# A graph kernel that gathers node rows: items of two chunks, rows as high and low halves, and a preparation that goes group by group

## The chip, the cores and the metric

The kernel runs on one core of a Trainium2 chip (trn2). The metric is the device time of one execution in microseconds. Before the change it is 2641.29 us, the median of 3 runs (2641.16 to 2641.54).

## What is computed

6250 nodes have 256 features each (x), and 200000 edges (src, dst) are sorted by their destination. With xn the layer norm of x, the result is

```python
x = x + gnn(edges, xn) + mix(xn)      # gnn: relu(segment_sum(h[src]*dinv[src]*dinv[dst], dst) + b), h = xn @ W, with self loops
x = x + ffn(layernorm(x))             # mix: linear attention over all nodes, two layer norms, a GELU layer
                                      # ffn: 8 experts, top-1 routing with a capacity, 256 -> 1024 -> 256
```

dinv is one over the square root of a node's number of incoming edges, its self loop among them. All values are float32.

## The kernel before

The nodes are 49 blocks of 128, the edges 1563 chunks of 128 consecutive edges (NCHUNK). The program has four stages, one after the other: `prepare`, `aggregate_and_mix`, `route` and `experts`. The change touches the first two.

`prepare` makes the table `node_rows` in DRAM, one row of 256 float32 per node (1024 bytes), which holds h times dinv of the node. ScalarE normalises a block of x (L455), TensorE transposes it (L530), ScalarE copies the transpose (L462), TensorE multiplies it by W in four records of a float32 product (L537), and ScalarE stores the result in `acc` (L471, L468). VectorE computes means and variances (L363, L364) of seven blocks at a time, called a group. The degrees come from the sorted destinations: GpSimd gathers one row of 128 destinations for each of the 49 blocks (`crow`, L303), VectorE counts in it (`compare`, L380 and L383), and from the places of the block ends (L396), shifted by one node on TensorE (L554, L555), come the degrees (L401) and dinv (L405 to L409). This is done once, for all 49 blocks together, when all `crow` rows have landed. 40 blocks have been stored without dinv by then and are scaled by VectorE (L413), nine are stored with it. SyncE writes the table in four transfers. At the end come the item lists: for 13 tiles of 128 chunks ScalarE, TensorE and VectorE turn the edge lists into columns (`src_chunk`, `dst_item`) and into the number of the chunk of every item (`chunk_item`, L436 to L440).

`aggregate_and_mix` does the edges. An item is one pair of a chunk and a block that has destinations in it; there are 1611. For every chunk GpSimd gathers the 128 rows of its sources with one indirect DMA (L680) into a slot of `ring`, which holds 32 chunks. Four chunks are a gang. SyncE waits until gang k has landed and raises `ready`, then waits until gang k-4 has been multiplied and raises `free`, for which GpSimd waits before it reuses the slots. For every item VectorE makes a 128x128 matrix of zeros and ones by comparing a column of destinations with 0 to 127 (`select`, L917), TensorE multiplies it with the gathered rows (L702, a float32 product in two records), and VectorE adds the result to the block's rows in `acc` (`add`, L930), four items later. Passes of 21 items (PER) hold the rest of the work between the items at fixed places: first the keys and values (four blocks per pass, 13 passes), then the attention and the hidden layer (one block per pass, 50 passes), then items alone. SyncE also fills `expert_rows` with empty rows, 7.9 MB in one transfer at gang 20 (L668), and a small one for the rest.

The order on each engine is that of the program; engines wait for one another by counting semaphores.

## Time and profile before

| | |
|---|---|
| median of 3 runs | 2641.29 us |
| the profiled execution's own time | 2633.95 us |
| its span | 2632.2 us |
| mean granted clock of TensorE | 0.864 |
| TensorE busy (matmul) | 1953.6 us, 74% |
| VectorE busy | 1718.5 us, 65% |
| ScalarE busy | 837.1 us, 32% |
| GpSimd busy | 1786.2 us, 68% |
| gathers of node rows | 1563 |

The times of the instructions come from the profiled execution, counted from the start of its span. Its own time is 1.75 us longer than its span and 7.34 us below the median of the other runs. Matmul records of one product overlap, so their mean duration is longer than the distance between two. "Issue" before an instruction is time in which its engine waited for nothing that the profile shows.

### The profile page before, as it was taken

The numbers are of one execution on the slowest core, as the hardware profiler recorded it, in microseconds if no ns is written. First come the engines' busy times: TensorE is split into PE (matmuls) and PEld (weight loads), VectorE is DVE, ScalarE is ACT, GpSimd is POOL, SyncE is SP. The second block draws the span as 40 slices with busy tenths as digits, with TensorE's granted clock in tenths as the row PEclk, the third lists the DMA queues.
The fourth block names the chain that finished last, engine by engine and source line by source line (L and its number), as shares of the span: only waits on it lengthen the run. The fifth ranks groups of instructions, "written<-read, shape, count | busy, mean of one in ns | idle before, by whom it ended". The sixth has DMA issues, their size and how long they took to land. (4 is left out here: it accounts for less than half of the span.)

```text
span 2632.2 us, 41321 instructions
## 1 busy us (share of the span) xinstructions
PE 1953.6 (74%) x8589; PEld 1434.4 (54%) x8589; DVE 1718.5 (65%) x5672; ACT 837.1 (32%) x1670; POOL 1786.2 (68%) x1893
## 2 busy tenths in 40 slices
PE   6785987777677777777767677766666575999996
PEld 4453554555455554555555455534333364888886
DVE  6553665666766666666666767655555593888885
ACT  5431332233233333333333333300000064544542
POOL 6276777777777777777777777777777553355354
PEclk9898999788888888888898978987777755999998
DMA  6336333333333333333333333333333333212320
GB/s 192 123 107 218 105 107 105 105 105 106 106 105 106 105 105 106 105 106 106 105 106 105 106 105 105 106 105 106 105 106 106 95 126 134 74 60 68 105 69 8
DMA packets 137976, 278.31 MB, mean 106 GB/s; under 512 B 34578, under 2 KB 81825, under 8 KB 137626
## 3 DMA queue, kind: packets, MB, share of 16 engines
q0 software_dynamic: 82144, 218.73, 28.6%
q1 hardware_dynamic: 55610, 57.09, 6.7%
q8 instruction: 83, 1.36, 0.2%
q14 instruction: 139, 1.14, 0.1%
HBM read 244.19 MB, written 35.50 MB: 106 GB/s over the span
## 5 line engine op out<-in xcount | busy, mean ns | idle before, releaser
L680 POOL DMA_INDIRECT ring<-node_rows,src_chunk x1563 | 1484.9, 950 | 483.0 <-issue 475.5
L702 PE MATMUL p_item<-ring,sel 128*128 x3222 | 1094.2, 469 | 543.6 <-SPq L650 438.8
L702 PEld LDWEIGHTS p_item<-ring,sel 128*128 128x128 f32 x3222 | 644.6, 225 | 907.3 <-issue 835.1
L930 DVE TENSOR_TENSOR acc<-acc,p_item 128x256 f32 (+1 forms) x1611 | 676.1, 420 | 668.7 <-PE p_item L702 596.6
L917 DVE TENSOR_SCALAR sel<-col,dst_item 128x128 f32<-128x128 f32 x1611 | 493.4, 307 | 0.5 <-PEq L167 0.5
L1437 POOL TENSOR_TENSOR low<-low,big 128x256 f32<-128x256 f32 x64 | 56.2, 879 | 173.0 <-DVE big L1617 172.5
L1551 PE MATMUL e_y<-w2h,hTh 128*128 128x256 f32 x512 | 148.7, 290 | 2.4 <-DVE hTl L1603 2.0
L1551 PE MATMUL e_y<-w2h,hTl 128*128 128x256 f32 x512 | 143.1, 279 | 0.0
L1551 PE MATMUL e_y<-w2l,hTh 128*128 128x256 f32 x512 | 142.9, 279 | 0.0
L1244 ACT ACTIVATE sdg<-mvg,eps_ln 128x7 f32<-128x7 f32 x7 | 2.1, 302 | 368.7 <-DVE mvg L1167 368.6
L1538 PE MATMUL e_f<-bTh,w1h 128*128 128x490 f32 (+1 forms) x256 | 99.8, 390 | 2.7 <-ACT hbuf L1486 2.7
L1551 PEld LDWEIGHTS e_y<-w2h,hTh 128*128 128x128 f32 x512 | 96.3, 188 | 4.4 <-DVE hTl L1603 3.8
L1538 PE MATMUL e_f<-bTh,w1l 128*128 128x490 f32 (+1 forms) x256 | 98.7, 385 | 0.0
L1538 PE MATMUL e_f<-bTl,w1h 128*128 128x490 f32 (+1 forms) x256 | 98.6, 385 | 0.0
L1486 ACT ACTIVATE hbuf<-e_f,fb_sb 128x490 f32<-128x490 f32 (+1 forms) x128 | 79.5, 664 | 57.1 <-DVE hTl L1603 36.4
L1428 POOL DMA_INDIRECT out_dram<-oo,rows x64 | 79.4, 1240 | 25.9 <-DVE oo L1594 16.8
L1551 PEld LDWEIGHTS e_y<-w2l,hTh 128*128 128x128 f32 x512 | 96.5, 188 | 0.0
L1551 PEld LDWEIGHTS e_y<-w2h,hTl 128*128 128x128 f32 x512 | 96.2, 188 | 0.0
L767 PE MATMUL p_q<-wq_sb,xnT_m 128*128 128x512 f32 x196 | 94.8, 607 | 0.0
L1123 POOL DMA_INDIRECT expert_rows<-acc,dest x49 | 57.6, 1176 | 52.6 <-DVE dest L1218 39.8
L853 ACT ACTIVATE x1T<-p_t,col_ln1b,col_ln1g 128x128 f32<-128x128 f32 x98 | 39.5, 453 | 169.1 <-PE p_t L733 169.1
L847 ACT ACTIVATE x1n<-t_m,nm,r 128x256 f32<-128x256 f32 x49 | 29.4, 600 | 179.0 <-DVE nm L980 179.0
(246 smaller groups left out, 2918.6 us busy)
## 6 DMA issues: line engine op xcount, KB each, us to landing
ring<-node_rows,src_chunk POOLq DMA_INDIRECT x1563
w1raw<-in_w SPq DMA_DIRECT2D x8, 1024.0 KB, 6.8
w2raw<-in_w SPq DMA_DIRECT2D x8, 1024.0 KB, 5.6
expert_rows<-empty SPq DMA_DIRECT2D x1, 7930.0 KB
rows<-expert_rows SPq DMA_DIRECT2D x8, 910.0 KB
res<-in_x SPq DMA_DIRECT2D x7, 896.0 KB, 11.0
out_dram<-acc SPq DMA_DIRECT2D x7, 896.0 KB, 4.1
node_rows<-acc SPq DMA_DIRECT2D x2, 1792.0 KB, 7.6
```

The lines of the kernel that those rows point to most:

```text
L680: nc.gpsimd.indirect_dma_start(ring[:, c % RING, :], None, table, bass.IndirectOffsetOnAxis(src_chunk[:, c:c + 1], 0)).then_inc(gathered[c ...
L702: pe.matmul(p_item[i % PSLOT][:, 0:C], sel[:, i % SELR, :], ring[:, bass.ds(c % RING, 1), :].rearrange("p a c -> p (a c)"), start=True, st ...
L767: mm = pe.matmul(p_kv, xnT[:, a, :], wq_sb[:, a, C:3 * C], start=(a == 0), stop=(a == CH - 1))
L853: nc.scalar.activation(x1T[:, a, :], p_t[:, a, :], ACT.Identity, scale=g["cols"]["ln1g"][:, a:a + 1], bias=g["cols"]["ln1b"][:, a:a + 1]). ...
L917: nc.vector.tensor_scalar(sel[:, i % SELR, :], col[:], dst_item[:, i:i + 1], None, ALU.is_equal).then_inc(selected, 1)
L930: nc.vector.tensor_tensor(a, a, p_item[j % PSLOT][:, 0:C], ALU.add).then_inc(added, 1)
L1123: nc.gpsimd.indirect_dma_start(slots, bass.IndirectOffsetOnAxis(dest[:, b:b + 1], 0), acc[:, b, :], None, bounds_check=SLOTS - 1, oob_is_e ...
L1428: nc.gpsimd.indirect_dma_start(out, bass.IndirectOffsetOnAxis(rows[0:r, u, t, C + 3:C + 4].bitcast(I32), 0), oo[0:r, t % 2, :], None, boun ...
L1437: nc.gpsimd.tensor_tensor(low[0:r, t % 2, :], low[0:r, t % 2, :], big[0:r, t % 2, :], ALU.add).then_inc(pool_st, 1)
L1486: nc.scalar.activation(hbuf[:, j % 2, h * NH[0]:h * NH[0] + NH[h]], p_f[(2 * j + h) % 4][:, 0:NH[h]], ACT.Relu, bias=fb1_sb[:, bass.ds(e, ...
L1538: mm = pe.matmul(p_f[c % 4][:, 0:NH[h]], w[:, a, j * P:(j + 1) * P], b[:, a, h * NH[0]:h * NH[0] + NH[h]], start=(q == 0), stop=(q == len( ...
L1551: mm = pe.matmul(p_y[t % 2][:, 0:C], h[:, j, t * P:(t + 1) * P], w[:, j, :], start=(q == 0), stop=(q == len(parts) - 1))
```

## The change

In `aggregate_and_mix` an item becomes a pair of two chunks and a block: 782 pairs, 830 items. The gathers stay one per chunk, but a row of the table is now 2048 bytes: the high half of each value (rounded to the format of single-pass products) and then the low half, the rest. An item is four single-pass products of 128x128 by 128x256 that add up in PSUM (two chunks, two halves). `select` makes two matrices in one operation, `add` stays one per item. The ring holds 24 chunks (6 gangs), KEEP and LAG are 3, SELR is 8, and a pass has 12 items with the other work at new places. The fill of `expert_rows` becomes 62 transfers of 128 rows, one at every fourth gang from gang 20.

In `prepare` the weights are centred (their column mean is taken off), so that x is transposed as it is and the product is scaled by rstd times dinv when it is stored. The counting of `crow`, the degrees and dinv go group by group, in eight groups, each before the stores of its blocks. ScalarE stores each block twice, rounded (high half) and full (`acc`), and VectorE subtracts for the low half. The halves stand in two buffers of four blocks (PIECE), and SyncE writes the table in 13 pieces. ScalarE waits for the piece two before to be written. The edge lists are transposed at the seams of groups 1 to 4, and the pair numbers come from one comparison and 13 products with a column of ones.

```diff
-PER = 21
+PER = 12
-NITEM = NCHUNK + NBLK - 1
+NITEM = NPAIR + NBLK - 1
-RING = 32
-SELR = 16
+RING = 24
+SELR = 8
-KEEP = 4
-LAG = 4
+KEEP = 3
+LAG = 3
-    table = nc.dram_tensor("node_rows", (NPAD, C), F32, kind="Internal").ap()
+    table = nc.dram_tensor("node_rows", (NPAD, 2 * C), F32, kind="Internal").ap()
...
+    CB = [0, 7, 14, 21, 28, 35, 42, 46, NBLK]
+    HELD = 3
+    PIECE = 4
+        def known(gi):
+            return (CB[gi] - 1 if gi else 0), (CB[gi + 1] - 1 if gi + 1 < NC else NBLK)
+        wanted = [max(CB[gi] - 1, 0) + HELD for gi in range(NC - 1)]
...
+            for k in range(NPIECE):                       # SyncE
+                lo, hi = k * PIECE, min(k * PIECE + PIECE, NBLK)
+                sp.wait_ge(high_ok, hi)
+                sp.wait_ge(low_ok, hi)
+                sp.dma_start(table[lo * P:hi * P, :].rearrange("(b p) c -> p b c", p=P),
+                             halves[:, k % 2, 0:hi - lo].rearrange("p b u c -> p b (u c)").bitcast(F32)
+                             ).then_inc(dma_tab[k % 2], 16)
...
+            centre_weights()                              # VectorE
+            means(0)
+            inverse_std(0)
+            means(1)
+            means(2)
+            inverse_std(1)
+            inverse_std(2)
+            for gi in range(NC):
+                positions(gi)
+                if gi + 3 < NG:
+                    means(gi + 3)
                 if gi > 0:
+                    low_halves(gi - 1)
+                degrees(gi)
+                if gi + 3 < NG:
+                    inverse_std(gi + 3)
+                inverse_degrees(gi)
+                if gi == NTB:
+                    pairs_passed()
+                if gi == NTB + 1:
+                    pair_numbers()
+            low_halves(NC - 1)
...
+            def store(b):                                 # ScalarE
                 s.wait_ge(h_ok, b + 1)
+                s.wait_ge(dinv_ok, group_of(b) + 1)
+                k = b // PIECE
+                wait(s, dma_tab[k % 2], 16 * (k // 2))
+                nc.scalar.activation(half(b, 0), h_slot(b), ACT.Copy, scale=rowscale[:, b:b + 1]).then_inc(high_ok, 1)
+                nc.scalar.activation(acc[:, b, 0:C], h_slot(b), ACT.Copy, scale=rowscale[:, b:b + 1]
+                                     ).then_inc(h_out, 1)
...
+            for b in range(NBLK):
+                copy(b)
+                if b in (1, 2):
+                    root(b)
+                for gi in range(NC - 1):
+                    if b == wanted[gi]:
+                        if gi + 3 < NG:
+                            root(gi + 3)
+                        if 1 <= gi <= NTB:
+                            as_floats(gi - 1)
+                        root_degree(gi)
+                        if 1 <= gi <= NTB:
+                            edge_columns(gi - 1)
+                if HELD <= b < NBLK - 1:
+                    store(b - HELD)
...
+            for b in range(NBLK):                         # TensorE
+                transposes(b)
+                if b > 0:
+                    products(b - 1)
+                for gi in range(NC - 1):
+                    if b == wanted[gi]:
+                        shift(gi)
+                        if 1 <= gi <= NTB:
+                            edge_columns(gi - 1)
+                        if gi == NTB + 1:
+                            pair_numbers()
...
-                pe.matmul(p_item[i % PSLOT][:, 0:C], sel[:, i % SELR, :],
-                          ring[:, bass.ds(c % RING, 1), :].rearrange("p a c -> p (a c)"),
-                          start=True, stop=True).then_inc(multiplied, 1)
+                rows = ring[:, bass.ds(q % (RING // 2), 1), :, :].rearrange("p a u c -> p (a u) c").bitcast(F32R)
+                for u in range(2):
+                    for part in range(2):
+                        mm = pe.matmul(p_item[i % PSLOT][:, 0:C], sel[:, i % SELR, u, :],
+                                       rows[:, u, part * C:(part + 1) * C], start=(u == 0 and part == 0),
+                                       stop=(u == 1 and part == 1))
+                mm.then_inc(multiplied, 1)
...
-                nc.vector.tensor_scalar(sel[:, i % SELR, :], col[:], dst_item[:, i:i + 1], None, ALU.is_equal
-                                        ).then_inc(selected, 1)
+                dst = dst_chunk[:, bass.ds(pair[i % (2 * QUAD)] * 2, 2)]
+                nc.vector.scalar_tensor_tensor(
+                    sel[:, i % SELR, :, :], dst.rearrange("p (u e) -> p u e", e=1).broadcast_to([P, 2, P]),
+                    nbase[:, bass.ds(block_of(i), 1)],
+                    col[:].rearrange("p (u e) -> p u e", u=1).broadcast_to([P, 2, P]), ALU.subtract, ALU.is_equal
+                    ).then_inc(selected, 1)
...
-                if k == 20:
-                    full = SLOTS // P
-                    sp.dma_start(slots[0:full * P, :].rearrange("(a p) c -> p a c", p=P),
-                                 empty[:].rearrange("p (a c) -> p a c", a=1).broadcast_to([P, full, ROW])
-                                 ).then_inc(dma_empty, 16)
-                    sp.dma_start(slots[full * P:SLOTS, :], empty[0:SLOTS - full * P, :]).then_inc(dma_empty, 16)
+                if k >= 20 and k % 4 == 0 and (k - 20) // 4 < NFILL:
+                    lo = (k - 20) // 4 * P
+                    rows = min(P, SLOTS - lo)
+                    sp.dma_start(slots[lo:lo + rows, :], empty[0:rows, :]).then_inc(dma_empty, 16)
```

## Rows read from the trace of the kernel before

**Rows 1.** The page's costliest groups: line, engine, operation, names, count, busy us, mean ns, idle before.

```profile
L680 POOL DMA_INDIRECT ring<-node_rows,src_chunk x1563 | 1484.9, 950 | 483.0 <-issue 475.5
L702 PE MATMUL p_item<-ring,sel 128*128 x3222 | 1094.2, 469 | 543.6 <-SPq L650 438.8
...
L930 DVE TENSOR_TENSOR acc<-acc,p_item 128x256 f32 (+1 forms) x1611 | 676.1, 420 | 668.7 <-PE p_item L702 596.6
L917 DVE TENSOR_SCALAR sel<-col,dst_item 128x128 f32<-128x128 f32 x1611 | 493.4, 307 | 0.5 <-PEq L167 0.5
```

**Rows 2.** Timeline of GpSimd: start us, length us; first gather, around 250 us, last.

```profile
121.27 1.03 POOL L680 DMA_INDIRECT ring<-node_rows,src_chunk  x1
...
245.22 0.95 POOL L680 DMA_INDIRECT ring<-node_rows,src_chunk  x1 [0.30 <-issue]
253.48 0.94 POOL L680 DMA_INDIRECT ring<-node_rows,src_chunk  x1 [7.32 <-SPq L657]
...
2087.98 0.95 POOL L680 DMA_INDIRECT ring<-node_rows,src_chunk  x1 [0.30 <-issue]
```

**Rows 3.** Operations by tile: minimum, median and maximum ns; landing of the 512-byte gathers.

```profile
L680 POOL DMA_INDIRECT ring<-node_rows,src_chunk x1563: 942/946/1194, 121.3 to 2088.0; - x196
...
L303 POOL DMA_INDIRECT crow<-in_dstR,chunk_i x49: 940/944/1709, 12.6 to 77.8; - x49
...
DMA to landing us min/median/max: 2.4/2.5/5.9
...
L1123 POOL DMA_INDIRECT expert_rows<-acc,dest x49: 971/973/3585, 2121.3 to 2205.1; - x49
```

**Rows 4.** Stretches: length, busy us (count) by engine, clock, DMA share, GB/s.

```profile
225.00:250.00 25.00, 5.60 (x22) 3.42 (x22) 4.80 (x16) 2.15 (x6) 16.08 (x17) 0.65 0.94 311
400.00:1000.00 600.00, 443.14 (x1764) 315.11 (x1764) 395.66 (x1467) 190.83 (x344) 454.68 (x478) 0.86 0.37 105
```

**Rows 5.** Timeline of SyncE's queue: the fill of the expert rows.

```profile
228.94 24.04 SPq L668 DMA_DIRECT2D expert_rows<-empty  x1
```

**Rows 6.** Groups by line from 400 to 1900 us.

```profile
L935 DVE SCALAR_TENSOR_TENSOR qT<-p_q,qe 128x256 f32<-128x256 f32 x49 | 19.9, 407 | 0.0
```

**Rows 7.** Timeline of TensorE in the experts' stage.

```profile
2400.11 0.28 PE L1551 MATMUL e_y<-w2l,hTh 128*128 128x256 f32 x1
2400.22 0.28 PE L1551 MATMUL e_y<-w2h,hTl 128*128 128x256 f32 x1
```

**Rows 8.** Timeline of the preparation, all engines' instructions by start.

```profile
12.56 1.13 POOL L303 DMA_INDIRECT crow<-in_dstR,chunk_i  x1 [9.00 <-DVE chunk_i L357]
...
82.61 0.21 DVE L396 SCALAR_TENSOR_TENSOR place<-chunk_f,count 128x49 f32<-128x49 f32 x1
...
85.50 0.21 DVE L409 TENSOR_TENSOR dinv<-dinv,tmp 128x49 f32<-128x49 f32 x1
...
86.50 0.47 ACT L468 ACTIVATE acc<-p_h,dinv 128x256 f32<-128x256 f32 x1
...
86.87 0.59 ACT L455 ACTIVATE xn<-res,nmr,rstd 128x256 f32<-128x256 f32 x1
...
87.20 1.91 PE L537 MATMUL p_h<-gw_sb,xnT 128*128 128x256 f32 x4
...
93.42 1.03 PE L537 MATMUL p_h<-gw_sb,xnT 128*128 128x256 f32 x4
...
119.78 0.27 DVE L440 TENSOR_SCALAR chunk_item<-p_row 1x128 int32<-1x128 f32 x1
```

**Rows 9.** Timeline of VectorE in the routing stage: seven statistics.

```profile
2101.47 2.38 DVE L1164 BATCH_NORM_STATS2 stt<-acc 128x6 f32<-128x256 f32 x7
```

**Rows 10.** Groups by line from 0 to 121 us: counting of a group.

```profile
L380 DVE TENSOR_TENSOR less<-crow,node_n 128x896 bf16<-128x896 int32 x7 | 7.7, 1105 | 14.0 <-DMA crow<-in_dstR,chunk_i 14.0
L383 DVE TENSOR_REDUCE count<-less 128x7 f32<-128x896 bf16 x7 | 7.6, 1086 | 0.2
```

**Rows 11.** DMA issues: count, KB each, median us to landing.

```profile
node_rows<-acc SPq DMA_DIRECT2D x2, 1792.0 KB, 7.6
```

More of the change, by code:

```diff
@@ L483, in _ @@
-            root(0)
-            root(1)
-            group(0, False)
-            with s.Fori(1, SG) as gi:
-                root(gi + 1)
-                group(gi, False)
-            for gi in range(SG + 1, NG):
-                root(gi)
-            s.wait_ge(deg_ok, 1)
-            nc.scalar.activation(dinv[:], deg[:], ACT.Sqrt).then_inc(deg_std, 1)
-            s.wait_ge(dinv_ok, 1)
-            for gi in range(SG, NG):
-                group(gi, True)
-            copy(NBLK - 1, GR - 1)
@@ new lines, in store, with as_floats @@
+                k = b // PIECE
[3 more added lines that the diff above has]
+                                     ).then_inc(h_out, 1)
+            def as_floats(k):
+                lo, hi = tiles(k)[0], tiles(k)[-1] + 1
+                s.wait_ge(dma_rows, 32)
+                for rows in (src_rows, dst_rows):
+                    nc.scalar.copy(rows[:, lo:hi, :].bitcast(F32), rows[:, lo:hi, :]).then_inc(rows_ok, 1)
@@ L508, in _ @@
+            root_degree(NC - 1)
+            for b in range(NBLK - HELD - 1, NBLK):
+                store(b)
+            s.wait_ge(listed, 2 * NTB)
         @block.tensor
@@ L524, in _, with transposes @@
             t_.wait_ge(dma_gw, 16)
-            def transposes(b, u):
-                t_.wait_ge(xn_ok, b + 1)
-                wait(t_, xnT_ok, b if u == 0 else b - 1)
+            for a in range(CH):
+                mm = pe.matmul(p_h[0][:, 0:C], ones[:], gw_sb[:, a, :], start=(a == 0), stop=(a == CH - 1))
+            mm.then_inc(mean_ps, 1)
+            t_.wait_ge(consts, 25)
+            def transposes(b):
+                t_.wait_ge(dma_x[b // GR], 16)
+                wait(t_, xT_ok, b - 1)
@@ L536, in products @@
                 for a in range(CH):
-                    mm = pe.matmul(p_h[u % 2][:, 0:C], xnT[:, u, a, :], gw_sb[:, a, :], start=(a == 0),
+                    mm = pe.matmul(h_slot(b), xT[:, b % GR, a, :], gw_sb[:, a, :], start=(a == 0),
                                    stop=(a == CH - 1))
                 mm.then_inc(h_ok, 1)
-            def group(gi):
-                for u in range(GR):
-                    b = gi * GR + u
-                    transposes(b, u)
-                    if not (isinstance(b, int) and b < 1):
-                        products(b - 1, (u - 1) % GR)
@@ L687, in _ @@
             t_.wait_ge(dma_w, 16 * NDMA_W)
-            regs = [t_.alloc_register(f"item_chunk{i}") for i in range(QUAD)]
-            chunk = []
+            regs = [t_.alloc_register(f"item_pair{i}") for i in range(QUAD)]
+            pair = []
             def item(it, k):
```

500 lines of the change are left out of this document (247 added, 253 removed).

## The prediction, made before the changed kernel ran

> **What bounds the kernel now.** I read the page first, then the timeline of GpSimd, the stretches with their DMA share, and last the first 121 us instruction by instruction. In the page's costliest groups the reader is to see that GpSimd issues one gather after the other and waits for nothing: 1563 gathers of 950 ns, and 475.5 us of "issue" between them, so 1.25 us from one to the next, 1968 us in all [rows 1]. TensorE waits most for SyncE, which signals that a gang has landed, and VectorE for TensorE. VectorE's two groups of item work fill 1170 of these 1968 us, TensorE's one 1094; neither sets the pace. The gathers run from 121.3 to 2088.9 us [rows 2], so the run is 121 us of preparation, 1968 us of gathers, and 543 us of routing and experts that nothing here touches. One edit can matter for each: when the first gather starts, what one gather costs, and what interrupts them. That an item now does two chunks halves work that is hidden.
>
> **The gathers.** Their number stays 1563. Each now fetches 128 rows of 2048 bytes. The trace has no such gather, so I bound it. Below: the 512-byte gathers of the preparation have a median of 944 ns, the 1024-byte ones 946 ns [rows 3]; on that line another 1024 bytes cost 4 ns, 6 us over 1563, or nothing if the 2 ns are noise. I take 2 us. Above: the scatter of 1040-byte rows has a median of 973 ns [rows 3], 27 ns more, which is 42 us if bytes were the reason. Since doubling once changed nothing, I stay at the low end.
>
> The bytes themselves: the gathers occupy the DMA engines 0.37 at 105 GB/s [rows 4], so twice the bytes is 0.74 if a byte keeps its price. A 512-byte gather lands 2.5 us after its issue [rows 3]. The ring shrinks from 8 gangs to 6, and with KEEP at 3 gang m is issued when gang m-3 has landed and gang m-6 is multiplied: 10 us of slack for landing, where there were 15. At 0.37 x 1.25 = 0.46 us more of transfer a gather stays far inside 10 us.
>
> The fill of the expert rows is one transfer of 24 us [rows 5]. It holds the gathers back so that GpSimd stands 7.3 us, the only stall in the stage [rows 2]. The 62 pieces of 130 KB, one every four gangs (20 us), are each under half a microsecond at the 311 GB/s of that stretch [rows 4]; the stall goes: -7.3 us. The same fill would cost it back if the engines ran at 1.0.
>
> Mean against median: 950 and 946 ns, and 944 for the gathers next to other work. (950-944) x 1563 = 9.4 us are lengthenings spread over the stage. The select, a one-input f32 operation at 307 ns [rows 1], becomes one scalar_tensor_tensor per item, and adds are halved. If these are what lengthens gathers, up to 9.4 us return; if not, none. I take 4. The Trainium skill, "SBUF — State Buffer", section "SBUF: two separate sides", says that a VectorE operation in a 2-port mode shuts GpSimd out so that it can't write descriptors, which would make the select a brake and the new form a release. The medians 944 and 946 speak against more than the 9.4 us.
>
> **Item work, hidden.** VectorE: 420 + 307 ns twice per pair of chunks [rows 1] becomes 420 plus a 128x256 scalar_tensor_tensor, 407 ns in this stage [rows 6]; 0.83 of each 2.36 us. TensorE: four single-pass products; such products follow each other in 0.12 us in the last stage [rows 7], 0.47 us per item, 0.94 at the lower of TensorE's two clock levels, against 2.36. The attention work per block moves from 21 slots of 1.22 us to 12 of 2.35, 28 us per pass in place of 26, with the same distances in time. 63 passes of 70 are used, so it ends before the gathers. Without that cover, one microsecond per pass would be 50 us. Cost: 0. The last pair adds about 0.5 us behind the last gather, since twice the bytes must land: +0.5.
>
> **The preparation.** Removed: 49 normalisations on ScalarE, 40 scalings on VectorE, and the item lists, thirteen tiles one after the other behind everything else, whose last operation ends at 120.05 us [rows 8]. Added: a second store per block on ScalarE (the high half), 49 subtractions on VectorE (the low half), eight rounds of positions, degrees and roots in place of one, and a table of 12.8 MB instead of 6.4. The chunk rows (49 gathers, the first at 12.56 us [rows 8], now without constants among them) end at 12.6 + 49 x 1.25 = 74 us and land by 76. The chain that I expect to end last is not that one but ScalarE's stores, which may start for a group only when its degrees are known:
>
> Start: after chunk_i at 12.3 us (the first chunk-row gather follows it) VectorE centres the weights (2.5 us with TensorE's product), then means of groups 0, 1, 2 (seven statistics in 2.38 us [rows 9] and seven short aggregates, an estimated 3 us each), three inverse deviations (1 us each), positions of group 0 (1.1 + 1.1 [rows 10] + 0.3), means of group 3, another deviation and the inverse degree: 12.3+2.5+9+3+2.5+3+1+1.2 = 34.5. First store at 35 us.
>
> Stores: two of 0.37 us from start to start and a copy of 0.27 (the spacing of such operations, 86.50 to 86.87 [rows 8]) is 1.01; TensorE needs about 1.2 per block (a product's four records take 1.03 when its clock is high [rows 8], and two transposes), against which three results are held. I take 1.11: 49 x 1.11 = 54.4 us.
>
> Seven seams between groups. At each, TensorE finishes the product that the last store freed (1.0), then does the shift (0.5), VectorE the degree (0.2), ScalarE the root (0.3), VectorE five linked steps of 0.2, and in four of them TensorE's eight transposes of the edge lists and ScalarE's two copies of 512 columns (1.3 + 1.2) come before the next store. The same steps over all blocks took 82.61 to 85.71 [rows 8]. So 4.4 us at four seams, 3.4 at two, 4.3 at the last: 28.7.
>
> Buffer of the halves: a piece of four blocks needs the piece two before it written out. VectorE makes low halves only after positions and means of the next group (5.5 us), and 1 MB takes 3 us plus 2 to land (1.8 MB: 7.6 [rows 11]). I place stalls at blocks 12 (2.9), 32 (3.4) and 40 (1.2): 7.5 us.
>
> End: low half 0.5, the last 1.25 MB 5.4, and 0.7 to the first gather. Sum 35+54.4+28.7+7.5+6.6 = 132.2. TensorE's clock: after the 5 us gap before 86 us its products take 1.91 us for four records and only from 93 on 1.03 [rows 8]; six seams with 3 us of idle bring some of this, +3.5 us. First gather at 136, bounds 125 (no stalls of the buffer, full clock) and 150 (every block at 1.4 us). Against 121.3: +14.7, from +4 to +29.
>
> **Sum**, against the profiled execution's own 2633.95 us: +14.7 -7.3 -4 +2 +0.5 = +5.9, 2639.9. The median of the runs is 7.3 above that execution, so 2647.2 for it.
>
> **Rivals.**
> *Preparation as fast as its gathers.* If a seam costs little, seven blocks (7.8 us) fit into the 8.75 of their seven gathers, and the end is 76 + about 8 for the last group + 6.6 = 91 to 105 at the first gather: -16 to -30. The list work that now ends at 120 speaks for it, since it is truly gone from the end. Against it: the seams are linked steps on three engines in order. It decides below 1.0 us per seam. With -8.8 in the stage: 2602 to 2617.
> *The descriptors cost by bytes.* 27 ns or more per gather: +42 us and up, about 2690. The equal medians speak against.
> *The wait moves to landing or to the block chain.* If a byte costs more than now, so that a gather's transfer passes 1.25 us (0.74 becomes 1.0), every gather follows it; 5% above is 98 us, 2740. Likewise if a pass of 12 slots needs more than 28.2 us; at 29 it is +40 us, 2690.
> *The change of select frees GpSimd.* All 9.4 us return: 2642; this lies inside my range. By the page of the Trainium skill named above this, or more, is to be expected.
> *No stall in the buffer and full clock:* 11 less than my forecast, 2636, the lower end of the spread.
>
> **How the numbers follow.** My forecast with its spread (preparation +4 to +29, stage -17 to -1): 0.72, its own range 2631 to 2668. Fast preparation 0.12. Bytes, landing or block chain 0.12. The other 0.04 is for what I have not seen. About 0.2% (5.3 us) is what a measurement tells from no change. Of the 0.72, 0.40 lies above 2646.6, 0.25 within, 0.07 below 2636. With the rivals and the rest: slower 0.40 + 0.12 = 0.52, same 0.25 + 0.02 = 0.27, faster 0.07 + 0.12 + 0.02 = 0.21. To leave out no more than 2 in 10 the range takes the slower half of the fast preparation: 2612 to 2670.
>
> **What would show it.** First gather at 136 us; ScalarE waiting for VectorE's dinv about 3 to 4 us seven times; waits of ScalarE on the node_rows DMA at blocks 12, 32, 40; gathers at 945 to 950 ns with 0.30 between; no stall near 250 us; DMA share near 0.75. I am wrong if the first gather starts before 120, if gathers are longer than 960 ns, or if GpSimd waits for SyncE again and again.

## The result, and the profile after

The changed kernel takes 2663.53 us (median of 4 runs, 2660.85 to 2664.48), the kernel before beside it on the same chip 2641.22 us (4 runs, 2637.89 to 2641.54). The ratio is 1.0086, 95% interval 1.0068 to 1.0103: slower by 22.3 us. I had forecast 2647 with a range of 2612 to 2670, and gave "slower" 0.52. The side and the range hold, but the sum is 16 us short. The profiled execution's own time is 2660.85 us, its span 2659.0 us, 26.8 us more than the 2632.2 us of before. The sum of the forecast, +5.9, was a sum of profile times, so in those it is 20.9 us short; the profiled execution of before lay 7.3 us below the median of its runs, that of the changed kernel 2.7.

First the page's costliest groups of the changed kernel, which answer to [rows 1].

```profile
L738 POOL DMA_INDIRECT ring<-node_rows,src_chunk x1563 | 1502.4, 961 | 537.6 <-issue 476.2
L763 PE MATMUL p_item<-ring,sel 128*128 x3320 | 821.1, 391 | 718.6 <-SPq L714 656.3
...
L998 DVE TENSOR_TENSOR acc<-acc,p_item 128x256 f32 (+1 forms) x830 | 345.8, 417 | 459.4 <-PE p_item L763 456.5
L987 DVE SCALAR_TENSOR_TENSOR sel<-dst_chunk,nbase,col 128x256 fp32r<-128x256 f32 x830 | 399.4, 481 | 143.4 <-issue 84.4
```

GpSimd is the bound as before: 1563 gathers with 476 us of issue between them. But a gather is 961 ns on the mean where it was 950 [rows 1], and the sum of their busy time went from 1484.9 to 1502.4 us. The two VectorE groups of item work fell from 1170 to 745 us, and nothing came of it, since they were hidden.

The operations by tile (minimum, median, maximum in ns, first and last start), against [rows 3]; then one stretch against [rows 4] (length, busy by engine, clock, DMA share, GB/s).

```profile
L738 POOL DMA_INDIRECT ring<-node_rows,src_chunk x1563: 942/949/1212, 135.8 to 2113.4; - x196
...
DMA to landing us min/median/max: 3.3/3.7/5.9
...
L353 POOL DMA_INDIRECT crow<-in_dstR,chunk_i x49: 943/947/1687, 11.5 to 73.4; - x49
```

```profile
400.00:1000.00 600.00, 378.02 (x1700) 305.28 (x1699) 289.95 (x898) 168.25 (x316) 455.22 (x475) 0.71 0.75 215
```

The median gather is 3 ns longer, the mean 11 ns: it is a few gathers that became much longer, not all of them a little. Twice the bytes give twice the GB/s at twice the share, as forecast. Last the timeline of GpSimd, against [rows 2]: the first gather, the place where the pause of 7.3 us was, the last one, and what follows it.

```profile
135.76 0.95 POOL L738 DMA_INDIRECT ring<-node_rows,src_chunk  x1 [61.42 <-POOLq L178]
...
245.77 0.94 POOL L738 DMA_INDIRECT ring<-node_rows,src_chunk  x1 [0.30 <-issue]
...
2113.42 0.95 POOL L738 DMA_INDIRECT ring<-node_rows,src_chunk  x1 [0.30 <-issue]
2120.31 0.18 POOL L1180 IOTA node_i<- 128x49 int32 x1 [5.94 <-POOLq L653]
```

These rows split the 26.8 us. The first gather moved from 121.3 to 135.8: +14.5. From the first to the last gather it was 1966.7 us and is now 1977.7: +10.9, which is +17.5 of gather time, +0.7 of issue, and -7.3 of the pause, which is gone. From the last gather's start to the end of the span: 544.2 to 545.6, +1.4. The first figure is what I forecast (+14.7), the third nearly so; the second I had at -9.3 (with +2 for the bytes). So the question for the experiments is what made the gathers longer.

The trace names a suspect. Here a stretch of 3 us of the changed kernel, GpSimd and VectorE, in order of start.

```profile
527.12 0.42 DVE L998 TENSOR_TENSOR acc<-acc,p_item 128x256 f32 x1
527.45 0.48 DVE L987 SCALAR_TENSOR_TENSOR sel<-dst_chunk,nbase,col 128x256 fp32r<-128x256 f32 x1
527.54 1.21 POOL L738 DMA_INDIRECT ring<-node_rows,src_chunk  x1 [0.30 <-issue]
...
528.60 0.49 DVE L987 SCALAR_TENSOR_TENSOR sel<-dst_chunk,nbase,col 128x256 fp32r<-128x256 f32 x1 [0.34 <-PE p_item L763]
...
529.06 0.95 POOL L738 DMA_INDIRECT ring<-node_rows,src_chunk  x1 [0.30 <-issue]
```

The gather at 527.54 starts 0.09 us after a selection and takes 1.21 us; it ends 0.82 us after that selection's end (527.93). The next one, at 529.06, starts 0.46 us after a selection, when only 0.03 us of it is left, and takes 0.95. I counted this over the 1563 rows of the timeline, which prints durations to 0.01 us. "Long" is 0.97 us or more; "excess" is the sum over all gathers of what they take above 0.945 us. The rounding raises the excess of before: by the busy times of the page, 1484.9 and 1502.4 us less 1563 x 0.945, it is 7.8 and 25.4 us.

```
                          long   mean of long   excess   beside the selection   beside the sum
                                    us            us      all     long           all    long
before                     87      1.025         10.5     228      62            457      0
changed                   150      1.083         24.8     284     136            231      0
```

"Beside" means that the operation runs 0.05 us after the gather's start. Of the changed kernel's 853 gathers that start beside no VectorE operation not one is long, and of the 231 beside the sum, which reads TensorE's result from PSUM, none. Of the 138 that start 0.10 to 0.35 us after a selection's start, 132 are long, by 0.04 to 0.23 us on the mean of those that start at the same place in it: the more of the selection is left, the longer. Not all of the 17.5 us is that: the long gathers beside the selection take 2.6 us above 0.945 in the kernel before and 18.2 in the changed one, and the median of all gathers went from 946 to 949 ns, some 4.7 us over 1563 (the later traces with 2048-byte rows have 946 or 947, so this part belongs to this execution or chip); beside other operations a little less was lost than before.

### The profile page after: what moved, and what is told of

It is laid out like the page before. It is cut to its first block and busy times, and to the rows that moved or that the text cites. A ratio compares the mean times of both kernels' runs of the same rounds, so it can differ in the third digit from the quotient of the medians.

```text
span 2659.0 us, 38729 instructions
## 1 busy us (share of the span) xinstructions
PE 1757.3 (66%) x8645; PEld 1454.1 (55%) x8645; DVE 1416.6 (53%) x4113; ACT 836.6 (31%) x1668; POOL 1803.9 (68%) x1892
## 5 line engine op out<-in xcount | busy, mean ns | idle before, releaser
L738 POOL DMA_INDIRECT ring<-node_rows,src_chunk x1563 | 1502.4, 961 | 537.6 <-issue 476.2
L763 PE MATMUL p_item<-ring,sel 128*128 x3320 | 821.1, 391 | 718.6 <-SPq L714 656.3
L763 PEld LDWEIGHTS p_item<-ring,sel 128*128 128x128 f32 x3320 | 637.5, 263 | 893.4 <-issue 884.9
L998 DVE TENSOR_TENSOR acc<-acc,p_item 128x256 f32 (+1 forms) x830 | 345.8, 417 | 459.4 <-PE p_item L763 456.5
L987 DVE SCALAR_TENSOR_TENSOR sel<-dst_chunk,nbase,col 128x256 fp32r<-128x256 f32 x830 | 399.4, 481 | 143.4 <-issue 84.4
L1003 DVE SCALAR_TENSOR_TENSOR kf<-p_q,ke 128x256 f32<-128x256 f32 x49 | 20.8, 425 | 216.4 <-ACT ke L947 216.4
L829 PE MATMUL p_q<-wq_sb,xnT_m 128*128 128x512 f32 x196 | 113.8, 711 | 0.0
L1073 DVE SCALAR_TENSOR_TENSOR kf<-p_q,ke 128x256 f32<-128x256 f32 x49 | 20.8, 425 | 151.7 <-ACT ke L900 151.7
L802 PE MATMUL p_g<-x1T,w1t_sb 128*128 128x128 f32 x392 | 94.6, 420 | 1.2
```

The source lines that it names most:

```text
L738: nc.gpsimd.indirect_dma_start(ring[:, c % RING // 2, c % 2, :], None, table, bass.IndirectOffsetOnAxis(src_chunk[:, c:c + 1], 0)).then_in ...
L763: mm = pe.matmul(p_item[i % PSLOT][:, 0:C], sel[:, i % SELR, u, :], rows[:, u, part * C:(part + 1) * C], start=(u == 0 and part == 0), sto ...
L802: mm = pe.matmul(p_g[:, m, :], w1t_sb[:, a, m * P:(m + 1) * P], x1T[:, a, :], start=(a == 0), stop=(a == CH - 1))
L829: mm = pe.matmul(p_kv, xnT[:, a, :], wq_sb[:, a, C:3 * C], start=(a == 0), stop=(a == CH - 1))
L987: nc.vector.scalar_tensor_tensor(sel[:, i % SELR, :, :], dst.rearrange("p (u e) -> p u e", e=1).broadcast_to([P, 2, P]), nbase[:, bass.ds( ...
L998: nc.vector.tensor_tensor(a, a, p_item[j % PSLOT][:, 0:C], ALU.add).then_inc(added, 1)
```

## Experiments

The runs stand on several chips, and each has its own runs of the kernel before. On the one of the result the kernel before takes 2641 us, on two of the experiments' 2638, on two others 3117 and 3119; what is different there is told at the end. Ratios are read only against the before of the same chip, and lengths of single gathers from the traces, where they are the same on all.

**The selection split in two operations.** This and the next three stand on a chip where before takes 3119 us.

```diff
-                nc.vector.scalar_tensor_tensor(
-                    sel[:, i % SELR, :, :], dst.rearrange("p (u e) -> p u e", e=1).broadcast_to([P, 2, P]),
-                    nbase[:, bass.ds(block_of(i), 1)],
-                    col[:].rearrange("p (u e) -> p u e", u=1).broadcast_to([P, 2, P]), ALU.subtract, ALU.is_equal
-                    ).then_inc(selected, 1)
+                base = nbase[:, bass.ds(block_of(i), 1)]
+                nc.vector.tensor_scalar(sel[:, i % SELR, 0, :], col[:], base, dst[:, 0:1], ALU.add, ALU.is_equal)
+                nc.vector.tensor_scalar(sel[:, i % SELR, 1, :], col[:], base, dst[:, 1:2], ALU.add, ALU.is_equal
+                                        ).then_inc(selected, 1)
```

> The changed kernel, its selection built by two 128x128 tensor_scalar operations per item (one for each chunk, (column + 128 x block) == destination, one tile input each) in place of one scalar_tensor_tensor of 128x256 with two tile inputs. Same values. In the changed kernel's trace all 145 gathers of the ring that took over 0.97 us (mean 1.083) began while VectorE ran an operation with two tile inputs, and the selection was the commonest of them. Theory A, the selection with two tile inputs holds back a gather that starts beside it: gathers over 0.97 us fall to about 60 or 90 in number, their excess over 0.945 us from 24.8 us to about 10, and the time by some 12 to 15 us, to about 2650. Rival B, rows of 2048 bytes make the gathers long (DMA share 0.75 instead of 0.37): no change, within 3 us of the changed kernel. Rival C, the longer VectorE time of two small operations (2 x about 0.33 against 0.48 us) delays items and frees: slower.

Measured: 3056.95 us against 3118.95, ratio 0.9837 (0.9794 to 0.9881), which says nothing of this edit, since the changed kernel itself wasn't run on that chip. The excess fell to 14.5 us, but 124 gathers are still long (mean 1.032), where theory A had 60 to 90. So a single tile input doesn't free them.

**High halves only.**

```diff
-    table = nc.dram_tensor("node_rows", (NPAD, 2 * C), F32, kind="Internal").ap()
+    table = nc.dram_tensor("node_rows", (NPAD, C), F32, kind="Internal").ap()
-        ring = sb("ring", [P, RING // 2, 2, 2 * C], st=st)
+        ring = sb("ring", [P, RING // 2, 2, C], st=st)
```

> The changed kernel with the table and the gathered rows of the high halves alone: it leaves the low halves out (1024-byte rows, 6.4 MB of table instead of 12.8, two products per item instead of four, no subtraction that makes the low half). Selection with two tile inputs unchanged. Theory A (the selection makes gathers long): the number of gathers over 0.97 us stays near 150 and their excess near 25 us; DMA share of the middle falls to about 0.37; the distance from the first to the last gather shrinks by 0 to 4 us only. Rival B (the bytes make gathers long): they fall to 90 or fewer and the stretch shrinks by about 13 us. For the preparation: the two waits for a buffer of the halves (2.1 and 1.7 us) go and the last piece lands sooner; first gather at about 128 to 132 us instead of 135.8, if the stores' pace (1.11 us a block) and the pauses between groups set the rest.

Measured: 3012.96 us, ratio 0.967 (0.963 to 0.9709). Half the bytes, and the gathers are as long as with all of them: 163 long, mean 1.089, excess 27.0 us. Here its group row.

```profile
L734 POOL DMA_INDIRECT ring<-node_rows,src_chunk x1563 | 1503.4, 962 | 872.8 <-issue 442.4 <-SPq L717 353.0 <-POOLq L178 77.5
```

The mean is 962 ns with 1024 bytes a row and 961 with 2048. The bytes are not the cause; that rival falls. Its first gather came at 165.1, that of the split selection, with the changed kernel's preparation, at 168.9: the low halves cost the preparation about 4 us, by one trace each (the same preparation varies by 1.4 us between traces, as told below).

**Before, with the fill in pieces alone.**

```diff
-                if k == 20:
-                    full = SLOTS // P
-                    sp.dma_start(slots[0:full * P, :].rearrange("(a p) c -> p a c", p=P),
...
+                if k >= 20 and k % 4 == 0 and (k - 20) // 4 < NFILL:
+                    lo = (k - 20) // 4 * P
+                    rows = min(P, SLOTS - lo)
+                    sp.dma_start(slots[lo:lo + rows, :], empty[0:rows, :]).then_inc(dma_empty, 16)
```

> The kernel before with one part of the change alone: the fill of expert_rows with empty rows goes in 62 pieces, one to every fourth gang from gang 20 on, in place of one large transfer. The trace of before has one pause of 7.3 us between two gathers near 250 us, while that fill (24 us) holds the queues. My theory: the pause goes and nothing else moves: 7 us faster, about 2634 us. Rival: the pieces, each 130 KB, hold single gathers' landings back and the gain is spread away again: same as before within 2 us.

Measured: 3105.87 against 3118.95, 0.9962 (0.9942 to 0.9981). There GpSimd waited for a free place 186 times, so the pause at the fill can't be told from the rest; the same edit stands on another chip below.

**Before, with two tile inputs in its selection.**

```diff
-                nc.vector.tensor_scalar(sel[:, i % SELR, :], col[:], dst_item[:, i:i + 1], None, ALU.is_equal
+                nc.vector.tensor_tensor(sel[:, i % SELR, :], col[:], dst_item[:, i:i + 1].broadcast_to([P, P]),
+                                        ALU.is_equal).then_inc(selected, 1)
```

> The kernel before with its selection written as a tensor_tensor of 128x128 with two tile inputs (the column numbers and the destination broadcast along the row) in place of a tensor_scalar with one tile input; same values, 1655 of them. Theory A (a VectorE operation with two tile inputs that runs when a gather starts makes it long): gathers over 0.97 us rise from 87 to over 150, their excess over 0.945 from 10.5 us to 20 or more, and the kernel is slower by 10 us or more, with rows of 1024 bytes as before. Rival B (bytes make them long): their number stays near 87 and the time within 3 us.

Measured: 3114.63 against 3118.95, 0.9993 (0.9971 to 1.0015): the same. My theory as written missed: 113 long gathers and not over 150, excess 11.8 us and not 20 (of the selections the trace has 1611, not 1655). What I read from it is the length. This selection takes 281 ns (the one of before 307, the changed one 481), 96 of the 188 gathers beside it are long, but only by 0.04 to 0.14 us on the mean, by when they start. So I gave the theory another form: a gather is held to the end of a VectorE operation that works in SBUF alone and is running when the gather starts, so what counts is how long that operation lasts. That form leaves something out: of the gathers beside the selection 51% are long here, 27% in the kernel before, and 30% (55 of 184) in the version with the fill in pieces on this same chip, though the operation is the shorter one. The second input counts too; the rows for both stand together further down.

**The selection's column numbers in PSUM.** If that is so, the same 0.48 us operation with one input in PSUM, like the sum, must hold nothing.

```diff
-PSLOT = 3
+PSLOT = 2
+        p_col = ps("p_col", [P, 4, P], st)
+            nc.vector.tensor_copy(p_col[:, 0, :], col[:]).then_inc(col_there, 1)
-                    col[:].rearrange("p (u e) -> p u e", u=1).broadcast_to([P, 2, P]), ALU.subtract, ALU.is_equal
+                    p_col[:, 0:1, :].broadcast_to([P, 2, P]), ALU.subtract, ALU.is_equal
```

> The changed kernel with the selection's column numbers read from a PSUM bank of their own in place of the tile col in SBUF; the bank comes from the items, which get two result slots instead of three. Values unchanged. In all traces so far no gather is long that starts beside the sum acc<-acc,p_item (SBUF and PSUM inputs, 0.42 us; 0 of 457 in the kernel before), while of the gathers that started 0.10 to 0.38 us after the changed selection began nearly all were held until it ended. Theory A (a VectorE operation that reads its tiles from SBUF alone and is running when a gather starts holds the gather to its own end): gathers over 0.97 us fall from 150 to 30 or fewer and the excess over 0.945 us from 24.8 to 5 us or less; if two slots cost nothing the time falls by 15 to 20 us against the changed kernel (to about 2645 where before is at 2641). Rival C (it is the length of the VectorE operation, wherever it reads): 136 gathers or more stay long beside the selection. Rival D: two slots make the items wait for the sums and ring places come free late: pauses between gathers, slower.

Measured: 2643.6 us (8 runs) against 2637.53 (13 runs), ratio 1.0024 (1.0014 to 1.0035). Against the changed kernel's 1.0086 that is 16 us less. The group rows of this kernel:

```profile
L739 POOL DMA_INDIRECT ring<-node_rows,src_chunk x1563 | 1484.4, 950 | 534.2 <-issue 475.8 <-POOLq L178 58.3
...
L991 DVE SCALAR_TENSOR_TENSOR sel<-dst_chunk,nbase,p_col 128x256 fp32r<-128x256 f32 x830 | 394.5, 476 | 139.3 <-issue 85.0 <-PE p_item L764 35.7 <-DVE p_col L974 0.9
```

The selection is as long as before the edit (476 ns), it runs as often, 286 gathers start beside it, and none of them is long. The gathers' time is back at 1484.4 us, what it was in the kernel before with half the bytes (1484.9 [rows 1]). 40 long ones are left, with an excess of 10.5 us (7.4 by the page's busy time), beside the block's other operations that read SBUF alone; I had expected 30 or fewer and 5 us. No pause came from the two result slots. Rivals C and D fall.

**The fill in pieces once more.**

> The kernel before with the fill of expert_rows in 62 pieces alone, once more: in the first call every kernel, the one before too (3119 us), ran in a state of the chip in which ring places came free late (pauses at 167 or more gathers), so that the pause of 7.3 us at the fill could not be read. Where before takes about 2641 us I expect 2634 (ratio 0.997); where it takes about 3119, a ratio of 0.996 to 1.000. Rival: the gain is spread away again, ratio 1.000.

Measured: 2628.92 us (5 runs) against 2637.53, ratio 0.9964 (0.9951 to 0.9978). The pause is gone and no other came:

```profile
L679 POOL DMA_INDIRECT ring<-node_rows,src_chunk x1563 | 1487.2, 952 | 476.2 <-issue 476.0
```

Idle before the gathers was 483.0 us [rows 1] and is 476.2: 6.8 us in the profile, 8.6 between the medians (I had expected 7). The rival falls.

**Both on the kernel before.** The fill in pieces and the column numbers in PSUM, on before's `tensor_scalar`.

> The kernel before with two small edits and nothing of the halves, pairs or group order: the fill in 62 pieces, and the selection's column numbers read from a PSUM bank of their own (two result slots instead of three). The pieces alone gave 2628.9 against 2637.5. Theory A: the 62 gathers held beside the selection in the trace of before go too, its excess of 10.5 us over 0.945 falls to about 4, and the time to about 2623 (ratio 0.9945). Rival D: an item of one chunk has only 1.19 us on the mean, two slots are too few, ring places come late and the kernel is slower than with the pieces alone.

Measured: 2627.23 us (5 runs) against 2637.95, ratio 0.996 (0.9947 to 0.9974), the fastest version of all, but not to be told from the pieces alone.

```profile
L680 POOL DMA_INDIRECT ring<-node_rows,src_chunk x1563 | 1483.0, 949 | 476.2 <-issue 476.2
...
L920 DVE TENSOR_SCALAR sel<-p_col,dst_item 128x128 f32<-128x128 f32 x1611 | 548.2, 341 | 0.0
```

Beside this selection 320 gathers start and none is long. The time of 2623 that I expected was missed: before had only 10.5 us of excess to give, 7.6 are left, and the first gather came 1.3 us later than with the pieces alone (122.28 and 120.95), so 4 us of gather time show as 1.7 between two medians that come from two chips. Rival D falls.

**Degrees out of the pauses between groups.** The preparation was the other large term.

```diff
                     if b == wanted[gi]:
-                        shift(gi)
+                        if gi == 0:
+                            shift(gi)
+                    if b == wanted[gi] + 2:
+                        shift(gi + 1)
...
-                        root_degree(gi)
+                        if gi == 0:
+                            root_degree(gi)
+                    if b == wanted[gi] + 3:
+                        root_degree(gi + 1)
```

> The changed kernel with the shift of the places (TensorE) and the root of the degrees (ScalarE) of every group but the first taken out of the pause between two groups and done two and three blocks after the previous pause; VectorE computes degrees and their inverses before the low halves. Everything else as in the changed kernel. In its trace the pauses between groups (3.0 to 3.5 us each beyond a block's pace) hold the chain shift, degree, root, reciprocal, while VectorE had the places 10 us before. Theory: the pauses shrink by 1 to 2 us each where that chain ends last, the first gather comes at 128 to 131 us instead of 135.8, and the whole is faster by as much. Rival E: the integer-to-float copies and the edge columns fill the same pauses on ScalarE (2 x 1.2 us), so that at most the last two pauses shrink: first gather at 133 to 135. Rival F: the low halves fall behind and their pieces land late: no gain, or later.

Measured: 2656.13 us against 2637.95, ratio 1.0074 (1.0059 to 1.0089), first gather at 134.7, 1.1 us earlier than in the changed kernel and not the 4.8 to 7.8 that I expected. The ratio can't be told from the changed kernel's 1.0086 (1.0068 to 1.0103). The 134.7 lies where rival E put it too, but the waits decide for rival F: what ScalarE waited for before its first store of a block (us, times):

```profile
  DMA node_rows<-halves: 13.9, 4
  DVE rowscale L445: 2.3, 2
```

In the changed kernel the same rows say 3.8 us in 2 waits and 5.5 us in 4. The wait for degrees went and the wait for a free buffer took its place.

**The split selection once more.**

> The changed kernel with the selection as two 128x128 operations with one tile input each, once more, since the first run of it came in the state of the chip where before took 3119 us. There the gathers over 0.97 us were 124 with a mean of 1.032 and the excess 14.5 us (24.8 in the changed kernel), held by operations of 0.36 us. Theory A as the runs since then have it (a gather is held to the end of the SBUF-only VectorE operation that runs at its start, so the length of that operation counts and not the number of its inputs): excess 13 to 16 us, the time 9 to 12 us below the changed kernel, ratio to before 1.0045 (2649 to 2652 where before is 2638 to 2641). Rival (two tile inputs are what holds a gather): excess 10 or less.

Measured: 2649.24 us (4 runs) against 2637.95, ratio 1.0041 (1.0026 to 1.0057), 12 us below the changed kernel. Excess 16.7 us, a little above my 13 to 16, far from the rival's 10; 111 of the 368 gathers beside the two operations are long. Its gathers take 1492.2 us in all, 10.2 less than the changed kernel's, and that is where the 12 us are, but for what two chips differ by.

Now the forms of the selection side by side (operations and their mean length, gathers that start beside it, how many are long, and what the long ones take above 0.945 us, together).

```
form of the selection                         ops     ns   beside   long    us
before, one SBUF input                       1611    307      228     62   2.6
before's, two SBUF inputs                    1611    281      188     96   6.1
before's, one input, in PSUM                 1611    341      320      0   0
split, one SBUF input (this run)             1660    362      368    111   6.2
changed, two SBUF inputs                      830    481      284    136  18.2
changed, one SBUF and one PSUM input          830    476      286      0   0
```

Both things count. From 281 to 481 ns, with two SBUF inputs in both, the loss triples with half as many operations; from one to two inputs, at 307 and 281 ns, it more than doubles. So "the length and not the number of inputs", as I wrote above, goes too far, and how much of the 12 us is the shorter operation and how much the single input is not told apart.

**Four places of two blocks, alone and with the degrees early, and all three together.**

```diff
-    PIECE = 4
+    PIECE = 2
-        halves = sb("halves", [P, 2, PIECE, 2, C], F32R, st)
+        halves = sb("halves", [P, 4, PIECE, 2, C], F32R, st)
```

> The changed kernel with the buffer of the halves cut otherwise: four places of two blocks (25 stores of two blocks to the table) in place of two places of four blocks (13 stores); same memory. ScalarE waited for a landed store 2.1, 1.7 and 0.2 us in the changed kernel. Theory: those 4 us go, and the last store is shorter: first gather at 130 to 132 us instead of 135.8, ratio to before about 1.007. Rival: the waits go but the pauses between groups take the time up, since the products are ready: no gain.

> The degrees taken out of the pauses (as in the run before that did so, where the waits for rowscale went but the waits for a landed store of halves grew to 4.6, 3.4, 2.6 and 3.2 us, first gather at 134.7) and the four places of two blocks together. Theory: the two waits stood in for each other; with both removed the first gather comes at 122 to 127 us, 8 to 13 us before that of the changed kernel, and the whole is faster by as much: ratio about 1.003 to 1.005. Rival: ScalarE's own work (49 blocks of 1.3 us with copies and edge columns) sets the end: first gather at 128 or later.

> The changed kernel with all three remedies: degrees early, four places of two blocks, column numbers in PSUM with two result slots. If the terms add up (column 16 us by the run of it, preparation 8 to 13 us), about 24 to 29 us below the changed kernel: 2630 to 2636 where before is 2638, ratio 0.997 to 0.999, which would put it beside or a little above the kernel before with its fill in pieces (0.9964). Rival: an earlier start of the gathers is lost again (a stall in the ring, longer gathers): above 1.000.

These ran where before takes 3116.71 us, and there the preparation starts late in every kernel: the first store of a block comes at about 62 us in place of 33. So I read them by the stretch from that store to the first gather, with the split selection (the changed kernel's preparation) on the chip of 3119 us as the base.

```
                                first store   first gather   between
changed (other chip)               33.2          135.8        102.6
degrees early (other chip)         33.7          134.7        101.0
split selection                    62.2          168.9        106.7
four places of two blocks          62.1          166.0        103.9
both                               63.1          160.1         97.0
all three                          62.7          155.7         93.0
```

Each alone gives 1.6 and 2.8 us, both together 9.7 (and 13.7 in the last row, whose third edit is not in the preparation, so 4 us is the uncertainty of such a reading). On the faster chips the changed kernel's preparation takes 102.1, 102.6 and 103.5 us in three traces, so the 1.6 alone is hardly more than that spread; and the four places brought 2.8 where I expected 3.8 to 5.8. The waits of ScalarE in the kernel with both:

```profile
  DVE rowscale L445: 2.8, 1
  DMA node_rows<-halves: 1.0, 1
```

The two waits stood in for each other, as expected. The ratios are 0.9831 (0.9794 to 0.9869), 0.9787 (0.9755 to 0.9818) and 0.9838 (0.9808 to 0.9869). My ratios for these three were for a chip where before takes 2638 and aren't tested by these. The third remedy brought nothing there: all three take 3063.13 us and both 3055.30, with ranges that overlap. That all three bring the change level with before is therefore only a sum: 2643.6 with the column in PSUM, less the 9.7, about 2634 with 4 us either way, above the 2627 of before with its small edits.

## Why the forecast was right in its side and short in its size

**Preparation, +14.7: measured +14.5, but by terms that made up for each other.** First store at 33.15 us (I had 35). The seven intervals across a seam are 4.10 to 5.41 us, together 33.1, so 25.3 beyond the block's 1.11 (28.7). Waits for a buffer 3.8 (7.5), at blocks 12 and 32 as placed, and none at 40. From the last store's end (129.94) to the first gather 5.8 (6.6). These are 9.8 us less than I had, and the block's pace outside the seams took them back: 67.7 us in place of 54.4 + 3.5. That two errors of 9.8 us cancel is luck. The timeline of ScalarE shows where.

```profile
34.50 0.49 ACT L522 ACTIVATE acc<-p_h,rowscale 128x256 f32<-128x256 f32 x1
36.64 0.37 ACT L514 COPY xT<-p_tr 128x256 f32<-128x256 f32 x1 [1.65 <-PE p_tr L586]
...
56.48 0.47 ACT L521 ACTIVATE halves<-p_h,rowscale 128x256 fp32r<-128x256 f32 x1 [2.13 <-DMA node_rows<-halves]
...
115.30 0.21 ACT L509 ACTIVATE dinv<-deg 128x4 f32<-128x4 f32 x1 [1.63 <-DVE deg L433]
116.67 0.47 ACT L521 ACTIVATE halves<-p_h,rowscale 128x256 fp32r<-128x256 f32 x1 [1.16 <-DVE rowscale L445]
```

After a seam ScalarE waits for TensorE's next transposes (16.3 us in 23 waits over the preparation). I had priced that as TensorE's clock alone, 3.5 us. The waits for degrees were 0.2 to 2.4 us each (7.6 us for deg in six, 5.5 for rowscale in four, of which one stands before the first store); only at the last three seams do the two together come to 2.8 to 3.6 us, near the 3 to 4 that I had put at all seven.

**The pause at the fill, -7.3: right.** The changed kernel has none, and the part alone on the kernel before is 8.6 us faster.

**Bytes, +2: they cost nothing in the gather.** 1484.4 us with 2048-byte rows, once the selection is out of the way, and 1484.9 with 1024-byte rows; the medians are 946 ns in both. A gather lands 3.7 us after its issue; nothing waited for that. **Tail +0.5:** measured +1.4.

**The selection, -4: this step failed, and with the wrong sign.** I asked whether one two-input operation in place of two one-input ones gives back up to 9.4 us of lengthenings. It gave none back and added: the gathers' time rose by 17.5 us, and 18.0 came back with the selection's column in PSUM. The mean gather is 961 ns, beyond the 960 that I had named as a sign of being wrong. I saw the 9.4 us and even the suspect, and erred in three ways. The 9.4 us were too many: I measured them from the 944 ns of the 512-byte gathers, while the long gathers beside the selection, all that a change of it could give back, held 2.6. I took the one-input operations for the only ones that hold a gather, while in the kernel before the two-input ones do it too; and I did not ask how long the new operation is. A gather beside the changed selection is lengthened only when it starts about 0.1 us or more into the operation and with 0.12 us or more of it left, by what is left beyond 0.12. Of 307 ns little remains after both (0.09 us), of 481 ns 0.26: half as many operations held 136 gathers in place of 62, and longer. The rule was read from this form and doesn't carry over as it is: it gives about 11 us for the split selection, where 6.2 were lost, and beside the two-input selection of 281 ns the holding begins at 0.03 to 0.05 us already. The bounds "nothing, or 9.4 us back" left out a loss, and so the likeliest value was too low. With the selection's column in PSUM the change costs 6.1 us, at the edge of the 5.3 that a measurement tells from no change, so "slower" came out as clearly as it did by a loss that I had not seen. (The bounds of the forecast's own terms, preparation and stage, give 2628 to 2669, where I wrote 2631 to 2668; the range given doesn't hang on it.)

The Trainium skill, "SBUF — State Buffer", section "Who interferes with whom", says that a VectorE instruction with two SBUF inputs contends with a GpSimd instruction that reads SBUF, and that one with at most one, outside the 2-port modes, doesn't. The first half agrees with this case's traces: 132 of 138 gathers held, and none with one of the inputs in PSUM (0 of 286). On the second half no run decides: before's selection with one SBUF input held 62 of 228, and no trace shows in which mode it ran. I had read only the rule on 2-port modes, from which the change looked like a release. The same section of the Trainium skill infers that a `tensor_tensor` doesn't stop the writing of descriptors. The runs neither show nor exclude it: a `tensor_tensor` selection lengthened 96 of 188 gathers, but only an operation that is on when the gather starts does so (of the 853 gathers that start beside nothing none is long, whatever starts after them). That it is the reading of the gather's index list which is held is my inference and was not tested.

**Of the rivals,** the fast preparation fell (135.8, not 91 to 105), the descriptor's price by bytes fell (961 and 962 ns at 2048 and 1024 bytes), the block chain and landing fell (no pause of GpSimd in the stage), and the release of GpSimd by the new selection fell with the wrong sign. TensorE's granted clock was 0.71 in the middle of the stage where it was 0.86 [rows 4], and is 0.70 in the 16 us faster kernel with the column in PSUM; it plays no part.

```profile
400.00:1000.00 600.00, 387.88 (x1721) 312.09 (x1720) 293.10 (x909) 170.60 (x321) 454.37 (x479) 0.70 0.75 216
```

## What to carry to other kernels

Where GpSimd issues gathers back to back, count the long ones and look at what VectorE runs at their start: a VectorE operation that works in SBUF alone has a price there, which in these runs was higher with two tile inputs than with one and grew faster than the length, so fusing two short ones into a long one can cost although it saves VectorE time. An operand in PSUM took the price away. When a wait is taken out of a chain with a small buffer behind it, look at the buffer at once: here the remedies alone gave 1.6 and 2.8 us and both 9.7, with up to 4 us of uncertainty. And try the small parts of a large change alone: the fill in pieces, the only part tried alone on the kernel before, paid 0.4%, while the whole lost 0.9%.

## What the runs showed that I had not expected

On two of the chips every kernel that ran there and elsewhere was 15 to 18% slower, and evenly so (before: 3103 to 3130 us in 34 runs). The lengths of the operations of GpSimd and VectorE are the same there: gathers 952 ns, sums 420 ns. What is different are waits in which no engine holds another by the records. Rows of the waits of before with the two-input selection (engine, line waited at, releaser, us, times, longest):

```profile
POOL ring L680 <- SPq L657: 455.2, 167, 17.6
...
DVE acc L930 <- remote: 429.8, 123, 17.6
```

VectorE stands for 3.5 us on the mean of these 123 waits, ring places come free late, and GpSimd waits 455 us for them. By that reading the item chain is the bound there in place of the gathers, which would fit that versions of the changed kernel are faster than before by 1.6% to 2.1% with its full work (and 3.3% with high halves only): fewer and larger items would pay. The changed kernel itself did not run there, and what causes the waits stays open; nothing here was run to tell.
